# The expansion of an inverted residual block as packed 32x32 products on image pairs, set between depthwise taps

## What is computed

```python
routing = sigmoid(mean(x, (2, 3)) @ wr.T + br)
h = einsum('bchw,oc->bohw', x, w1)               # expansion, 16 -> 96 channels
h = relu6(bn(h, g1, b1, m1, v1))
h = depthwise_conv_3x3(h, wd)                    # 9 taps a channel, padding 1
h = relu6(bn(h, g2, b2, m2, v2))
k = einsum('be,eoc->boc', routing, we)
x = x + bn(einsum('bchw,boc->bohw', h, k), g3, b3, m3, v3)
```

## Time and profile before

| what | us |
|---|---|
| runs of the kernel, median of 3 | 813.12 |
| lowest and highest run | 810.16, 816.64 |
| profiled execution, span from first to last instruction | 806.4 |
| TensorE busy in it | 637.5 |
| VectorE busy | 566.1 |
| ScalarE busy | 493.9 |

### The profile page before, as it was taken

One profiled execution on the slowest core, in us unless ns is written; L12 is line 12 of the kernel. 1 busy time (PEld: TensorE's weight loads), 2 busy tenths in 40 slices (PEclk: granted clock), 3 DMA queues, 4 the chain that ended last, 5 costly groups with the idle time before them and its releaser, 6 DMA issues.

```text
span 806.4 us, 30382 instructions
## 1 busy us (share of the span) xinstructions
PE 637.5 (79%) x13948; PEld 430.9 (53%) x13948; DVE 566.1 (70%) x771; ACT 493.9 (61%) x692; POOL 134.9 (17%) x229
## 2 busy tenths in 40 slices
PE   3539999999998668888888588859888888649392
PEld 1215555557885347656665465537666556426161
DVE  6995252211243699999999743889999999784466
ACT  2725343432331589999999341498999999341513
POOL 1000000000005323333320003523333320000000
PEclk9869999999999979999999879989999999969596
DMA  4000000000017987888872007987888872000002
GB/s 174 0 0 3 2 3 2 3 17 4 4 35 204 365 278 269 262 262 258 259 253 107 2 3 192 320 310 257 276 257 274 260 248 112 2 1 4 1 3 105
DMA packets 28778, 108.73 MB, mean 135 GB/s; under 512 B 10612, under 2 KB 15412, under 8 KB 24552
## 3 DMA queue, kind: packets, MB, share of 16 engines
q0 software_dynamic: 14400, 86.80, 32.0%
q1 hardware_dynamic: 14248, 19.97, 8.1%
HBM read 91.84 MB, written 19.65 MB: 138 GB/s over the span
## 4 chain that ended last, share of the span: by engine, by line
PE 48%; ACT 29%; DVE 14%; issue 8%; DMA 1%; SPq 0%; ACTq 0%; DVEq 0%
PE psum L1278 14%; PE psum L1325 11%; ACT arena L1113 7%; ACT arena L1123 6%; PE psum L1254 6%; ACT arena L1112 5%; PE psum L1359 4%; PE psum L1474 4%; ACT arena L1096 4%; ACT arena L1103 3%; PE psum L1383 2%; PE psum L1337 2%; PE psum L1291 2%; PE psum L1481 1%; DVE arena L750 1%
## 5 line engine op out<-in xcount | busy, mean ns | idle before, releaser
L1359 PE MATMUL psum<-arena 64*64 64x198 f32 (+4 forms) x4512 | 231.4, 346 | 56.8 <-DVE arena L751 45.2
L1359 PEld LDWEIGHTS psum<-arena 64*64 64x64 f32 x4512 | 172.8, 136 | 122.6 <-DVE arena L751 61.4
L1278 PE MATMUL psum<-arena 32*32 32x512 f32 x3456 | 115.0, 597 | 0.3 <-DVE arena L673 0.3
L1550 POOL DMA_DIRECT2D arena<-offsets_by_batch x128 | 79.6, 636 | 207.3 <-DVE arena L751 141.4
L1123 ACT ACTIVATE arena<-psum 128x792 f32<-128x792 f32 (+1 forms) x96 | 97.2, 1012 | 15.3 <-PE psum L1364 9.0
L1325 PE MATMUL psum<-arena 32*32 32x512 f32 x2304 | 87.4, 651 | 21.9 <-issue 15.9
L749 DVE SCALAR_TENSOR_TENSOR arena<-arena 128x792 f32<-128x792 f32 (+3 forms) x96 | 92.6, 964 | 12.7 <-ACT arena L1113 11.4
L1113 ACT ACTIVATE arena<-arena 128x792 f32<-128x792 f32 (+3 forms) x96 | 101.3, 1056 | 0.0
L1112 ACT ACTIVATE arena<-arena 128x792 f32<-128x792 f32 (+3 forms) x96 | 101.0, 1052 | 0.0
L1278 PEld LDWEIGHTS psum<-arena 32*32 32x32 f32 x3456 | 73.4, 103 | 39.9 <-issue 13.8
L751 DVE SCALAR_TENSOR_TENSOR arena<-arena 128x792 f32<-128x792 f32 (+3 forms) x96 | 92.3, 962 | 0.0
(11 more groups left out here) (149 smaller groups left out, 702.3 us busy)
## 6 DMA issues: line engine op xcount, KB each, us to landing
arena<-offsets_by_batch POOLq DMA_DIRECT2D x112, 576.0 KB, 7.9
arena<-offsets_by_batch POOLq DMA_DIRECT2D x16, 624.0 KB, 7.7
offsets<-arena SPq DMA_DIRECT2D x32, 256.0 KB, 8.6
offsets_by_batch<-offsets SPq DMA_DIRECT2D x184, 24.0 KB
arena<-columns POOLq DMA_DIRECT2D x24, 160.0 KB, 9.6
columns<-arena POOLq DMA_DIRECT2D x8, 320.0 KB, 6.7
arena<-in_x SPq DMA_DIRECT2D x4, 512.0 KB, 5.5
out<-arena SPq DMA_DIRECT2D x8, 256.0 KB, 2.2
```

The source lines that it names most:

```text
L1278: ins = t_.matmul(ps_q(j, dw_bank(t, half) + i), cols(W_DIAG + (t * K + k) * Q, Q, Q * i, Q), ap(T_PAD[t % 4] + row * PW + k % 3, [[PW, CR ...
L1359: ins = t_.matmul(ps_t(s, bank + r, first * K * w, many * K * w), window, ap(g_at(unit, d0) + first * TW + s * w, [[GS + TW, many], [SLOTS ...
```

## The change

- **Weights.** The 96 columns "w1" leave the shared weights; VectorE no longer builds W_HID. Instead a new input of 128 x 768 (384 KB) is loaded by SP into W_HID, behind the shared weights. For tile 0 it is what VectorE built. For tiles 1 to 5, group j's columns hold the weights in all four 32-partition groups, in the 16 rows of the image of that parity.
- **Spreads.** A pair of images is 32 partitions. For each of 4 pairs and 8 chunks a transfer of 32 x 512 values (64 KB) brings the pair's chunk to partition group chunk mod 4, into `XR = T_HID[4]`, which is free then. SP issues pairs 0 and 2, GpSimd pairs 1 and 3, each as soon as L634 has finished the chunk. Four chunks of a pair then lie under one another on 128 partitions.
- **Expansion.** Tile 0 keeps its 8 products of 128x128. For tiles 1 to 5 four chunks are a block of 16 products of 32x32 by 512 columns: i the chunk, j the hidden group.
- **Order.** The 12 halves are steps 0 to 11. Steps 0 to 9 hold the block of the same half one tile on (`BLOCKS`), issued before tap 3 of the nine, in step 2 before tap 6. The routing product stands before tap 3 of step 2, the wait for its bias before tap 6.
- **Banks.** A step's depthwise uses one set of four banks, its block the other set, in which the next step's depthwise then runs. TensorE waits at tap 3 until ScalarE has read the previous half, and at a step's start until ScalarE has read the previous block.
- **ScalarE and VectorE** follow that order. Pooling of the channels comes before step 0's work, the mixing of the experts after step 2's clip.

```diff
-for name, width in [("gate", C), ("upd", C), ("w1", HID), ("wr", E),
+for name, width in [("gate", C), ("upd", C), ("wr", E),
+TENSOR_HALVES = tuple((t, half) for t in range(NT) for half in range(2))
+BLOCKS = tuple(((t + 1, half),) if t + 1 < NT else () for t, half in TENSOR_HALVES)
+ROUTE_STEP = 2
+FIRST_TAP, SECOND_TAP = 3, 6
-        def dw_bank(t, half):
-            return 0 if t >= 4 and half == 1 else 4
+        def dw_bank(step):
+            return 0 if (len(TENSOR_HALVES) - 1 - step) % 2 == 0 else 4
+        def blocks_before(step):
+            return 2 + sum(len(blocks) for blocks in BLOCKS[:step])
+        XR = T_HID[4]
+        def spread_pair(pair, half):
+            return XR + (2 * pair + half) * CH
...
+            sp.dma_start(cols(W_HID, NT * P), hidden_weights).then_inc(s_hw, 16)
...
+            for pair in (0, 2):
+                for ch in range(NCH):
+                    sp.wait_ge(s_xsum, ch + 1)
+                    sp.dma_start(cols(spread_pair(pair, ch // 4), CH, Q * (ch % 4), Q),
+                                 cols(XIN + ch * CH, CH, Q * pair, Q)
+                                 ).then_inc(s_xr0[ch // 4] if pair == 0 else s_xr2, 16)
...
-            by_image(W_HID, "w1", HID).then_inc(s_w1, 1)
...
+            hidden(0, 0, dw_bank(0))
+            hidden(0, 1, dw_bank(1))
+            for step in range(len(TENSOR_HALVES)):
+                if step == ROUTE_STEP:
                     act.wait_ge(s_rl, 1)
                     a.activation(cols(ROUT, B * E), cols(ROUTL, B * E), ACT.Sigmoid).then_inc(s_rsig, 1)
+                for t, half in BLOCKS[step]:
+                    hidden(t, half, dw_bank(step + 1))
+                depthwise_relu(step)
...
+            def first_hidden():
+                for ch in range(NCH):
+                    pe.wait_ge(s_xsum, ch + 1)
+                    t_.matmul(ps(dw_bank(ch // 4) + ch % 4, 0, CH), cols(W_HID, P), cols(XIN + ch * CH, CH), start=True,
                               stop=True).then_inc(s_c1, 1)
+            def hidden(t, half, bank):
+                pe.wait_ge(s_relu, 4 * (2 * t + half))
+                if t < 3:
+                    pe.wait_ge(s_xr0[half], 64)
+                    pe.wait_ge(s_xr1[half], 64)
+                else:
+                    pe.wait_ge(s_xr2, 128)
+                    pe.wait_ge(s_xr3, 128)
+                for i in range(4):
+                    for j in range(4):
+                        pair = (4 * t + j) // (2 * NG3)
+                        ins = t_.matmul(ps_q(j, bank + i), cols(W_HID + t * P + Q * j, Q, Q * i, Q),
+                                        cols(spread_pair(pair, half), CH, Q * i, Q), start=True, stop=True)
+                    ins.then_inc(s_c1, 1)
+            def depthwise(step):
+                t, half = TENSOR_HALVES[step]
+                if step >= 2:
+                    pe.wait_ge(s_dwa, 4 * (step - 1))
+                if step >= 1:
+                    pe.wait_ge(s_relu, 4 * blocks_before(step))
                 pe.wait_ge(s_clip, 2 * t + half + 1)
+                pending = list(BLOCKS[step])
                 for k in range(K):
+                    if k == FIRST_TAP:
+                        if step >= 1:
+                            pe.wait_ge(s_dwa, 4 * step)
+                        if step == ROUTE_STEP:
+                            route(dw_bank(step + 1))
+                    if k == SECOND_TAP and step == ROUTE_STEP:
+                        pe.wait_ge(s_rl, 1)
+                    if pending and k == (SECOND_TAP if step == ROUTE_STEP or len(pending) < len(BLOCKS[step]) else FIRST_TAP):
+                        hidden(*pending.pop(0), dw_bank(step + 1))
...
+            first_hidden()
             pe.wait_ge(s_diag, NT)
+            for step in range(len(TENSOR_HALVES)):
+                depthwise(step)
...
+            for pair in (1, 3):
+                for ch in range(NCH):
+                    pool.wait_ge(s_xsum, ch + 1)
+                    g.dma_start(cols(spread_pair(pair, ch // 4), CH, Q * (ch % 4), Q),
+                                cols(XIN + ch * CH, CH, Q * pair, Q)
+                                ).then_inc(s_xr1[ch // 4] if pair == 1 else s_xr3, 16)
             pool.wait_ge(s_zp, 64)
```

More of the change, by code:

```diff
@@ L124, in constants, with build @@
     return c, entries
-def build(nc, x, const, entries, vectors, weights, offset_weights, out):
+def build(nc, x, const, entries, vectors, weights, offset_weights, hidden_weights, out):
     with ExitStack() as ctx:
@@ L1032, in _ @@
             act.wait_ge(s_padz, 1)
-            def hidden(t, chunks):
+            def hidden(t, half, bank):
                 if t == 3:
                     act.wait_ge(s_zp, 64)
-                for ch in chunks:
+                if t >= 4:
+                    act.wait_ge(s_dw, 4 + 4 * max(step for step, part in enumerate(TENSOR_HALVES) if part[0] == t - 4))
+                for i in range(4):
+                    ch = 4 * half + i
                     act.wait_ge(s_c1, NCH * t + ch + 1)
-                    a.activation(pad_rows(T_PAD[t % 4], ch * CR + 1, 1), ap_ps(ch % 4, [[W, CR], [1, W]]),
+                    a.activation(pad_rows(T_PAD[t % 4], ch * CR + 1, 1), ap_ps(bank + i, [[W, CR], [1, W]]),
@@ L1242, in _ @@
             pe.wait_ge(s_blend, NCH)
-            pe.wait_ge(s_w1, 1)
+            pe.wait_ge(s_hw, 16)
             pe.wait_ge(s_g_act, NCH)
-            def hidden(t, chunks):
-                for ch in chunks:
-                    n = NCH * t + ch
-                    if n >= 4:
-                        pe.wait_ge(s_relu, n - 3)
-                    if t == 0:
-                        pe.wait_ge(s_xsum, ch + 1)
-                    t_.matmul(ps(ch % 4, 0, CH), cols(W_HID + t * P, P), cols(XIN + ch * CH, CH), start=True,
-                              stop=True).then_inc(s_c1, 1)
@@ L1611, in layout @@
     wrep("upd", per_image(f(i["L0_conv_upd_w"]).T))
-    wrep("w1", per_image(f(i["L1_conv_w1"]).T))
     wrep("wr", per_image(f(i["L1_conv_wr"]).T))
@@ L1629, in layout @@
         wrep(f"cn{n}", per_image(cen))
-    return vectors, weights, offset_weights
+    w1 = f(i["L1_conv_w1"])
+    hidden_weights = np.zeros((P, NT, 4, Q), np.float32)
+    for t in range(NT):
+        for j in range(4):
+            image, group = divmod(4 * t + j, NG3)
+            rows = np.arange(P) // C == image if t == 0 else np.arange(P) // C % 2 == image % 2
+            hidden_weights[rows, t, j] = np.tile(w1[Q * group:Q * (group + 1)].T, (rows.sum() // C, 1))
+    return vectors, weights, offset_weights, hidden_weights.reshape(P, NT * P)
 def kernel(**inputs):
```

88 lines of the change are left out of this document (34 added, 54 removed).

## The result

| | before | changed |
|---|---|---|
| median of the runs, us | 812.43 (4 runs, 810.16 to 816.64) | 782.63 (4 runs, 774.98 to 783.58) |
| span of the profiled execution, us | 806.4 | 781.8 |
| TensorE, VectorE, ScalarE busy, us | 637.5, 566.1, 493.9 | 608.9, 564.6, 492.5 |

The ratio is 0.962, with an interval of 0.958 to 0.966: 30 us faster. Forecast were 786.7 us and a range of 782.5 to 791.5, so the forecast is 4.1 us too high and the median stands at the range's lower edge.

A forecast was written before the change was run, and what follows sets the result against it. TensorE was taken as the bound, back to back from 68.30 to 212.33 us. -22.1 - 4.8 - 0.3 + 0.8 = -26.4 against span 806.4 gave 780.0; with 6.7 carried over, 786.7 us, range 782.5 to 791.5.

The forecast's parts named there:

- the 6.7 us carried over between span and runs: Whole kernel: runs' median 813.12 against span 806.4; the 6.7 us difference was added to the forecast span unchanged.
- the 0.8 us for the clock: New TensorE idle gap before the first tap: lowered clock to cost 0 to 2.3 us, 0.8 taken.
- the stretch behind the projection: Everything after the projection's start: claimed as long as before; growth over 2 us would show the forecast wrong.
- Stretch from first tap to projection: Depthwise and packed expansion on TensorE: 144.03 us to become 121.9, a gain of 22.1.
- The first tap: Start of the depthwise products: from 68.30 to 63.47, 4.83 us earlier, with VectorE's clip next in the way.
- The front: VectorE's chain before the expansion: the blend moves up from 19.15 to 18.81, 0.3 us won, bound 0.95.
- Spreads at nothing: The 32 transfers of 64 KB: taken to cost 0, bounds 0 and +3.4 us; first block covered by 1.3 us.
- Rival 1: Spreads land late and hold TensorE at tap 3 of the first half: +3.4 + 1.5, about 791 us; chance 0.09.
- No wait at the blocks: TensorE at the packed blocks: no stall taken, with slack of 1.1 us at tap 3 for ScalarE's clearing.
- rivals 3 and 4: At the blocks: late bank handover to ScalarE, 822 us at x = 3.5, chance 0.03; small stalls, 791.7 us, chance 0.12.
- Rival 2: Blocks of sixteen 32-row products don't pack and cost 3.43 us as before: 810.7 us, no change; chance 0.04.
- the two like rows: Two earlier TensorE gaps: after 2.03 us idle the clock was 1.00, after 2.01 it stood at 0.50.

## Why the prediction was right, and where it missed

The mechanism held: TensorE's stretch shrank as reckoned, by the packing, with no wait at the blocks. Three terms of the sum failed, all to the same side: the 6.7 us carried over between span and runs, the 0.8 us for the clock, and the stretch behind the projection, put down as unchanged.

- **Stretch from first tap to projection, 144.03 to 121.9 forecast:** 121.42. The prices were right: less 12 halves of 9.23 and 0.84 for the routing, 9.8 us are left for ten blocks, 0.98 each (1.03 taken), and the shape change is gone. The unpacked blocks put both back and cost 31.0 us.
- **The first tap, 63.47 less the 0.3 of the front, 63.17:** 63.34 came, with VectorE's clip as the next bound, as said. Taking the diagonals off VectorE moved the tap to 61.1 and, with nine products ahead, to 60.3: VectorE was the bound, and the products the next.
- **The front, -0.3:** the blend moved by 0.2, and the first tap of the two profiles by 4.96 in all against the 5.1 of both terms.
- **Spreads at nothing:** right, by more room than given: 2.2 us to land, not 9.9. Rival 1 never came near. Its upper bound of 3.4 us doesn't follow from its own words: 55.4 and twice 9.9, less the 66.6 at which the block asks, are 8.6.
- **No wait at the blocks, rivals 3 and 4:** 1.8 us of idle in all 3456 records, none at a block. The slack at tap 3 is real, about 1.0 us of the 1.1; the stall came when the block was moved two taps forward.
- **Rival 2:** the blocks pack.
- **The clock, +0.8, failed:** behind a gap of 1.75 us the first step ran at clock 1.00 and took 10.30 us. Nothing was paid. Of the two like rows the first was the right one here. That was not sure to be so: with 24 added waits TensorE idled 2.59 us behind the nine unused products, its clock then fell to 0.50 and the eight products took 8.93 us in place of 7.83. The same kernel's busy times and clock, in the columns of the first step's view above:

```profile
53.70:56.50 2.80, 2.80 (x5) 1.07 (x4) 2.80 (x4) 1.22 (x2) 1.46 (x4) 0.50 0.63 151
```

- **Up to the projection:** 184.76 came, 212.33 - 26.4 = 185.9 was forecast: 0.8 of the clock, 0.5 of the stretch, 0.15 back at the start.
- **The 6.7 us "outside the span or in the spread of the runs" failed as well:** each run of these two kernels is its span plus 1.8 or 1.9. The rest, 4.9 us, was one short execution (806.4) set against a median of three (813.12); over 83 runs the mean is 811.4. With 1.7 less for the baseline the forecast would have been 785.0.
- **Behind the projection "as long as before":** the means leave 596.8 us before (811.4 - 1.8 - 212.8) and 594.5 changed (781.1 - 1.8 - 184.8), each known to about 0.8. This last 2.3 us isn't settled. In the profiled pair it is the other way round, 594.1 before and 597.0 changed: that is 2.9 us more, and more than 2 was named as a sign of being wrong. But a single pair doesn't decide it: the kernel before gave 601.0 when profiled again, and the changed kernel's three profiled executions were 2.5 to 6.0 us longer than the mean of the other runs beside them. Neither TensorE's alignment nor one of VectorE's gaps is shown to explain the 2.3 us.

Against the runs' mean of 781.1 the miss is 5.6 us: 1.7 of baseline, 0.8 of clock, 0.8 of small terms ahead of the projection and 2.3 behind. The range was too narrow below: it counted the runs' scatter at 2.5 us, and a place behind the change that differs by some us between kernels and even between runs wasn't in it. Its terms added up give 782.8 to 792.4, not 782.5 to 790. That the median of four runs came out at 782.63, just inside, is luck: the mean of all 16 is 781.1.

## What to carry to other kernels

When an engine runs back to back, products that use the whole array poorly are worth reshaping into the tile shape of their neighbours: sixteen small products fitted into the stream at the neighbours' own price (1.03 us), and the change of shape between them, 0.66 us a time, went too. Place such a block where the banks it needs are already cleared and its own reads still end before the next user: here tap 3 of nine (tap 6 once, in step 2), and two taps earlier or five later cost 1.1 and 1.7 us a step. Before adding a profiled span to a median of runs, ask for the run's own time beside the span: here the difference is 1.8, and the rest is the scatter of executions.

## What the runs showed that was not expected

- A transfer of 64 KB inside the on-chip memory lands 2.0 to 2.2 us after its issue, on SP's and on GpSimd's queue alike.
- GpSimd's products of two tiles (1.12 us each, 6.71 for six) slow VectorE's scans from 1.22 to 1.53 us and its two-tile multiplies from 1.05 to 1.52, and leave its read of PSUM alone.
- TensorE kept clock 1.00 behind the idle gap ahead of the first tap in all three profiles of the changed kernel, with gaps of 1.75, 1.23 and 2.37 us behind the eight products. It fell to 0.50 in the kernel with 24 added waits, after a gap of 2.59 us behind nine products.
- Idle gaps marked "issue" were waits for instructions: on TensorE 0.7 to 4.3 us each in layer 2's opening, ending 1.2 to 1.7 us after a 16,384-byte instruction packet lands, and on VectorE some 3 us, with a packet of 8,192 bytes inside, that come and go with a handful of waits that are already met. Of 2.9 us won ahead of the projection with the diagonals on ScalarE none is seen at the end; that these gaps took it back is not shown.
